# Second cross attention of a two-layer decoder: other chunks for the projections of the batch after next

## The reference

```python
x = x + _L1_xattn_ref(_layernorm(x, axis=-1), ctx_1024, ctx_1024, ...)
...
qh = _split_heads(q @ W_q.T + b_q, bs)
kh = _split_heads(k @ W_k.T + b_k, bs)
vh = _split_heads(v @ W_v.T + b_v, bs)
scores = jnp.einsum('bhqd,bhkd->bhqk', qh, kh) / jnp.sqrt(jnp.float32(D_K))
weight = jax.nn.softmax(scores, axis=-1)
attn = jnp.einsum('bhqk,bhkd->bhqd', weight, vh)
```

## Time and profile before

| what | value |
|---|---|
| runs | 1430.25, 1433.26, 1434.88 us, median 1433.26 |
| the profiled execution | 1429.79 us, span 1428.0 us |
| TensorE / VectorE / ScalarE / GpSimd busy | 95% / 75% / 61% / 54% of the span |
| second cross attention, first to last scores | 901.8 to 1317 us |
| granted TensorE clock, mean of the span | 0.984 |
| one batch of twelve chunks there | about 27 us |

### The profile page before, as it was taken

One profiled execution on the slowest core, in us unless ns is written; L12 is line 12 of the kernel. 1 busy time (PEld: TensorE's weight loads), 2 busy tenths in 40 slices (PEclk: granted clock), 3 DMA queues, 4 the chain that ended last, 5 costly groups with the idle time before them and its releaser, 6 DMA issues.

```text
span 1428.0 us, 25410 instructions
## 1 busy us (share of the span) xinstructions
PE 1356.4 (95%) x9220; PEld 1012.2 (71%) x9220; DVE 1065.1 (75%) x2128; ACT 864.0 (61%) x1849; POOL 767.4 (54%) x431
## 2 busy tenths in 40 slices
PE   7889999999999999999998987899999999999898
PEld 4648888888888888888866754555556556555687
DVE  6458778888777887778844677677777777776787
ACT  4437667666667666667623553566666666665575
POOL 5026443334444444442260291588888888885363
PEclk9899999999999999999999999999999999999999
DMA  3132222211212222221150123446446446420331
GB/s 85 61 91 52 57 57 57 55 43 36 49 52 58 57 51 57 57 57 36 43 151 15 57 64 80 115 104 139 106 101 138 110 95 139 94 66 1 87 105 45
DMA packets 71803, 104.39 MB, mean 73 GB/s; under 512 B 14670, under 2 KB 54934, under 8 KB 71550
## 3 DMA queue, kind: packets, MB, share of 16 engines
q1 hardware_dynamic: 60062, 91.39, 25.6%
q10 hardware_dynamic: 11616, 11.38, 3.0%
HBM read 63.65 MB, written 2.11 MB: 46 GB/s over the span
## 4 chain that ended last, share of the span: by engine, by line
PE 79%; DVE 11%; DMA 3%; ACT 2%; issue 2%; SPq 1%; POOL 1%; ACTq 0%; DVEq 0%; POOLq 0%
PE PS L701 9%; PE PS L1104 6%; PE PS L715 6%; PE PS L689 5%; PE PS L690 5%; PE PS L691 5%; PE PS L1118 5%; PE PS L717 5%; PE PS L716 5%; PE PS L1084 5%; PE PS L1043 3%; PE PS L1049 3%; DMA inv_kept<-row_inv 2%; PE PS L744 2%; DVE QO_area L1399 2%
## 5 line engine op out<-in xcount | busy, mean ns | idle before, releaser
L1233 POOL TENSOR_TENSOR QO_area<-QO_area,prob_a 125x896 f32<-125x896 f32 x150 | 315.1, 2101 | 22.7 <-ACT prob_a L1325 3.2
L867 ACT ACTIVATE HL<-PS 125x512 fp32r<-125x512 f32 (+1 forms) x384 | 206.8, 539 | 177.8 <-PE PS L701 160.7
L959 DVE TENSOR_TENSOR HL<-PS,HL 125x512 fp32r<-125x512 f32 (+1 forms) x384 | 238.0, 622 | 74.6 <-ACT HL L867 53.5
L1399 DVE TENSOR_REDUCE QO_area<-PS 112x1 f32<-112x500 f32 x384 | 238.9, 670 | 60.3 <-PE PS L1084 60.2
L1325 ACT ACTIVATE prob_a<-PS 125x448 f32<-125x448 f32 x384 | 187.5, 540 | 103.9 <-PE PS L1104 100.5
L774 POOL TENSOR_TENSOR HL<-ctx_area,ones 125x512 fp32r<-125x512 f32 (+1 forms) x64 | 93.1, 1454 | 247.3 <-PE PS L717 189.3
L715 PE MATMUL PS<-HL 125*128 125x512 f32 (+1 forms) x384 | 155.7, 405 | 2.4 <-DVE HL L959 2.0
L689 PE MATMUL PS<-HL 128*128 128x500 f32 x336 | 153.1, 456 | 4.7 <-DVE HL L929 3.9
L1104 PEld LDWEIGHTS PS<-HL 98*125 98x125 f32 x768 | 102.9, 186 | 71.4 <-ACT prob_a L1325 37.9
L877 ACT ACTIVATE prob_a<-prob_a,neg_max 128x500 f32<-128x500 f32 x192 | 135.5, 706 | 26.7 <-DVE neg_max L951 25.4
L1084 PE MATMUL PS<-HL 96*112 96x500 f32 x384 | 129.4, 408 | 17.9 <-DVE QO_area L1399 15.3
(11 more groups left out here) (262 smaller groups left out, 2743.3 us busy)
## 6 DMA issues: line engine op xcount, KB each, us to landing
HL<-prob_b SPq DMA_DIRECT2D x128, 187.5 KB, 4.0
ctx_area<-in_ctx_T SPq DMA_DIRECT2D x16, 750.0 KB, 13.4
ctx_area<-in_ctx SPq DMA_DIRECT2D x16, 750.0 KB
HL<-ctx_area SPq DMA_DIRECT2D x64, 187.5 KB, 3.8
inv_area<-in_ctx_T SPq DMA_DIRECT2D x8, 750.0 KB, 4.1
prob_a<-in_ctx_T SPq DMA_DIRECT2D x8, 750.0 KB, 4.7
inv_area<-inv_kept ACTq DMA_DIRECT2D x16, 256.0 KB, 3.5
ctx_area<-in_L_ffn_W SPq DMA_DIRECT2D x16, 256.0 KB, 3.4
```

Of the source, the lines that this page charges most:

```text
L867: nc.scalar.activation(pH[k % 3][0:KC, 0:width(g)], PS[0:KC, 2 + k % 3, 0:width(g)], ACT.Copy)\
L959: nc.vector.tensor_tensor(pL[k % 3][0:KC, 0:width(g)], PS[0:KC, 2 + k % 3, 0:width(g)], pH[k % 3][0:KC, 0:width(g)].bitcast(fp32), ALU.sub ...
L1233: nc.gpsimd.tensor_tensor(late_acc[b % 2], before, late_p[n % LATE_P], ALU.add).then_inc(m["padd"], 1)
L1399: nc.vector.tensor_reduce(late_part[b % 2][:, u // NKB, u % NKB:u % NKB + 1], PS[0:2 * S, u % NKB, 0:KB], AX, ALU.max).then_inc(m["mx"], 1)
```

## The change

A table of chunks takes the place of the conditions in all three loops. Keys stay in three pieces and values in three; each moves to another pass, on TensorE, ScalarE and VectorE alike, and `queries` moves from c = 5 to c = 7. No instruction is added or taken away. Line numbers behind the inserted two lines are higher by two in the changed kernel.

```diff
+        K_CHUNKS, V_CHUNKS = (2, 4, 6), (8, 9, 10)
+
...
-                    if b + 2 < B and c in (2, 3, 4):
-                        project(b + 2, c - 2)
-                    if b + 2 < B and c in (6, 8, 10):
-                        project(b + 2, c // 2)
+                    if b + 2 < B and c in K_CHUNKS:
+                        project(b + 2, K_CHUNKS.index(c))
+                    if b + 2 < B and c in V_CHUNKS:
+                        project(b + 2, 3 + V_CHUNKS.index(c))
...
-                    if b + 2 < B and c in (2, 3, 4):
-                        keys(b + 2, c - 2, 7)
-                    if b + 2 < B and c in (6, 8, 10):
-                        values(b + 2, c // 2 - 3, 7)
-                    if b + 2 < B and c == 5:
+                    if b + 2 < B and c in K_CHUNKS:
+                        keys(b + 2, K_CHUNKS.index(c), 7)
+                    if b + 2 < B and c in V_CHUNKS:
+                        values(b + 2, V_CHUNKS.index(c), 7)
+                    if b + 2 < B and c == 7:
                         queries(b + 2)
...
-                    if b + 2 < B and c in (2, 3, 4):
-                        keys(b + 2, c - 2, 7)
+                    if b + 2 < B and c in K_CHUNKS:
+                        keys(b + 2, K_CHUNKS.index(c), 7)
```

## The result

| | kernel before | changed kernel |
|---|---|---|
| median | 1431.76 us (4 runs) | 1481.74 us (4 runs, 1472.19 to 1484.84) |
| ratio | | 1.0331, 95% interval 1.0293 to 1.0369 |
| profiled execution, span | 1428.0 us | 1481.7 us |
| granted TensorE clock, mean | 0.984 | 0.950 |

It is slower, as forecast, but by 50 us and not by 11: outside the range of 1438 to 1459, and even above the 1471 of the rule that stood beside the clock rival.

The account below looks back on a forecast made before the run. TensorE's own instructions bound the projection chunks checked, with bank 7 waits between key pieces; afterwards the late stack would bind. Stack waits +11.1, first batch +0.7, tail -0.9: +10.9 on 1433.3 gives 1444 us, range 1438 to 1459.

Parts of the forecast that it names:

- the rule that stood beside the clock rival: Skill's rule on short idles: every wait followed by a slow stretch, 14 x 1.9 = 27 us, an estimated 1471 us.
- the clock rival: TensorE's clock falls behind seven of the 14 stack waits, 1.9 us each: +13, so 1457 us; chance 0.26.
- That the stack bounds the new order: Chunk 0: TensorE waits for a stack of 12.9 us; period 27.74 us against 26.89, 13 x 0.85 = +11.1 us.
- That the bank waits go and the values cost nothing: Chunks 2 to 10: bank 7 waits between key pieces vanish, 0.54 us less a batch; neighbouring value chunks cost nothing extra.
- That the first 1.06 us of the wait are free: Chunks 0 to 2: VectorE splits during the wait, so maxima to chunk 2 scores take 2.88 us, not 3.94.
- The clock falls after the waits: Slow TensorE clock behind seven of the 14 stack waits, 1.9 us each: +13, so 1457 us; chance 0.26.
- The tail: After the last batch's 1270.47: the covered split lets the last GpSimd adds start earlier, -0.9 us.
- the 7.6 us that the change was after: Bank 7 waits between key pieces removed, 0.54 us in each of 14 batches: -7.6 us.

Follow-up runs that it names:

- Experiment 1: Changed kernel with two throwaway matmuls ahead of TensorE's wait for the stack in chunk 0: 1441.36 us, ratio 1.0068.
- experiment 3: Kernel before with values moved to chunks 8, 9, 10 and queries to chunk 7, keys left in 2, 3, 4: 1430.40 us, ratio 0.9982.
- experiment 8: Changed kernel with keys in chunks 2, 4 and 5, so the stack starts one chunk later than in the kernel before: 1427.48 us, ratio 0.9967.
- experiment 9: Keys in chunks 2, 4, 5 and values in 8, 9, 10, plus one throwaway matmul ahead of the stack wait: 1423.12 us, ratio 0.9937.
- experiment 6: Kernel before with two of eleven GpSimd adds a batch cut to 16 columns: 1420.02 us, ratio 0.9922.
- experiment 7: Kernel before with one operand of the subtraction in split_maxima moved to PSUM bank 7, all adds kept: 1418.29 us, ratio 0.9893.
- experiment 4: Kernel before, old order, with only the stack held back until the scores of chunk 7: 1508.69 us, ratio 1.0564.
- experiment 2: Changed kernel with one throwaway matmul ahead of TensorE's wait for the stack in chunk 0: 1454.88 us, ratio 1.020.

## Why the prediction was wrong

- **That the stack bounds the new order**: right. 14 waits as forecast, 30.1 us of them against about 33; the stack 12.84 us in the batch shown, 12.9 in the mean, against 12.9; the period with the clock up 27.6 to 27.7 against 27.74. Experiment 1 has this case by itself at 1441 us, against my 1444.
- **That the bank waits go and the values cost nothing**: right, chunk by chunk, and experiment 3 for the values.
- **That the first 1.06 us of the wait are free**: right in time, 2.91 against 2.88 us, but only while the clock holds (experiments 8 and 9).
- **"The clock falls after the waits"**: this is the step that failed. The sum that gave 1444 has the clock up all the way and puts this term at nothing; it was 35 us in the 13 periods, and the 40 us that experiment 1 gave back. The mechanism was named as a rival; its chance (0.26) and its size were wrong. I had 7 of 14 waits followed by a fall at 1.9 us each, 13 us. It was 12 of 14, at 3.1 us, and the last one alone lasted 20.4 us. The error in the price was to halve the slow stretch of the earlier trace rows "since dense work follows": the new ones mostly lasted the full 6.8 us. In the chance, I set much by one row, the wait of 0.87 us at 920.92 that left the clock up, for waits more than twice as long.
- **The tail**, -0.9: it was +6.7, from the long slow stretch. In experiment 1, with the same order and no such stretch there, it was -2.0. Behind the last projections the loop is leaner (chunks of 1.64 us with the clock up), and there the low clock stayed for seven chunks.
- **The Trainium skill's rule** that stood beside that rival ("TensorE: Matmul & The Clock Gate", section "A second HAM failure mode: psum-queue depth-cycling", on frequent short idles between groups): the trace agrees with it for these waits, 12 of 14, and not for the shorter ones of experiment 1, none of 14; the 1471 that I made of it with the same 1.9 us was too low for the same reason.
- **What I passed over**: the end of `split_maxima`. I read its 1.86 us in the earlier trace rows as its own time, though the trace has the same operation at 0.26 us in one batch and 0.17 in another. In the kernel before it was worth 12 to 15 us (experiments 6 and 7), more than the 7.6 us that the change was after.

## What to carry to other kernels

Before work is spread out, ask what starts behind its last piece: a transfer of nearly 13 us, due only 1.2 us after its landing, set the latest chunk for the last key piece, and no busy share showed it. Price a new wait on TensorE with the clock behind it, not only by its length; where it can't be avoided, throwaway matmuls in it gave back 40 of 50 us here. A bank wait is better removed by another bank than by moving the work.

## What the runs showed of the hardware

- Idle of 2.8 to 3.8 us a batch in dense work (experiment 4) went with a fall of TensorE's clock to 0.50 fourteen times in 14, idle of 1.9 to 2.5 us (the changed kernel) twelve times, idle of 1.3 us in the mean (experiment 2) five times, and of 0.7 us in the mean (experiment 1) never. In experiment 8 it was also 0.7 us in the mean, and the clock fell three times, behind waits of 1.08, 1.29 and 1.95 us; waits of 1.35 us (experiment 1) and 1.64 us (experiment 2) were followed by no fall. So the length of the wait alone does not decide it, and which of like waits is followed by a fall I can't tell from these runs.
- A slow stretch in dense work cost 3.1 us for 6.8 us at half clock.
- A VectorE subtraction of two small SBUF operands lasted until GpSimd's running add of 2.1 us ended: 1.86 us, 1.13 or 0.26, by the phase between the two. With one operand in PSUM it took 0.17 us beside the same adds. It was worth 15 us of this kernel (experiment 7).
- Twelve SBUF to SBUF copies of 187.5 KB took 12.8 us from first issue to last landing, the same with the next load right behind them.
